# Mixture-of-experts matmuls fed through one shared PSUM bank: two slots per pass instead of one

## The reference

```
xn = layernorm(x)
p  = xn @ Wv.T + bv                      # 16 heads of 8; q = k = v = p
s  = softmax(q k.T / sqrt(8)) v          # per batch and head, 1024 x 1024 scores
s  = s @ Wo.T + bo
z  = layernorm(xn) * g + b               # router and experts see z
w  = top-2 of softmax(z @ rW + rb) over 8 experts, normalised
hid_e = gelu(z @ W1[e] + b1[e])          # 128 -> 256, exact gelu
out_e = hid_e @ W2[e] + b2[e]            # 256 -> 128
f  = xn + sum_e w_e * out_e
out = x + s * silu(f)
```

## Time and profile before

| | us |
|---|---|
| median of 3 runs | 629.17 (628.3 to 630.58) |
| the profiled execution | 632.46 |
| its span | 630.7 |

### The profile page before, as it was taken

The page is one execution under the profiler, slowest core; times in us unless marked ns, Lnnn a source line. Parts: engine busy times, 40 slices in busy tenths (PEclk is TensorE's granted clock), DMA queues, the critical chain, the costliest instruction groups (busy, mean ns, idle before and its releaser), DMA issues.

```text
span 630.7 us, 11527 instructions
## 1 busy us (share of the span) xinstructions
PE 571.2 (91%) x3990; PEld 232.3 (37%) x3990; DVE 240.1 (38%) x695; ACT 543.2 (86%) x591; POOL 230.1 (36%) x252
## 2 busy tenths in 40 slices
PE   3778884799999999799999999999988999999996
PEld 2553320223344344333444344434334343433221
DVE  5553863573333333113222232223232852223381
ACT  4576663699999999979999999999999999999994
POOL 2364047827777774254211121112203334341000
PEclk9977776799999999869999999999995999999999
DMA  6137697746466655227363445453233654442220
GB/s 164 45 101 219 231 304 276 184 132 149 110 162 133 162 96 116 70 67 160 68 153 99 127 112 132 103 135 108 70 117 108 173 167 139 130 116 83 65 66 19
DMA packets 100989, 81.54 MB, mean 129 GB/s; under 512 B 54219, under 2 KB 92638, under 8 KB 100318
## 3 DMA queue, kind: packets, MB, share of 16 engines
q1 hardware_dynamic: 94270, 71.26, 43.2%
q0 software_dynamic: 6656, 9.48, 4.8%
HBM read 58.07 MB, written 28.39 MB: 137 GB/s over the span
## 4 chain that ended last, share of the span: by engine, by line
PE 74%; ACT 9%; DVE 7%; issue 5%; DMA 4%; SPq 1%; ACTq 0%; DVEq 0%
PE bank_v L1330 35%; PE pair L1276 16%; PE bank_f L1370 8%; PE bank_f L1379 8%; ACT exps L776 7%; DMA p_dram<-w_ring 3%; PE bank_f L1347 2%; PE pair L1236 1%; ACT pre L752 1%; PE bank_f L1343 1%; PE pair L1227 1%; DMA x_tok<-in_L_attn_x 1%; DVE o_turned L1082 1%; PE bank_f L1354 1%; DVE v_tok L863 1%
## 5 line engine op out<-in xcount | busy, mean ns | idle before, releaser
L776 ACT ACTIVATE exps<-pair 128x1024 f32<-128x1024 f32 x512 | 488.9, 1049 | 54.6 <-PE pair L1276 36.3
L1330 PE MATMUL bank_v<-exps,v_tok 128*32 128x512 f32 x2048 | 285.0, 630 | 3.1 <-ACT exps L776 1.6
L687 POOL DMA_INDIRECT o_dram<-o_ring,slot_place x80 | 77.4, 968 | 238.3 <-DVE o_ring L1133 238.0
L1276 PE MATMUL pair<-q_ring,k_ring 26*128 26x512 f32 x1024 | 152.9, 513 | 2.7 <-ACT exps L776 2.1
L1276 PEld LDWEIGHTS pair<-q_ring,k_ring 26*128 26x128 f32 x1024 | 60.7, 188 | 93.4 <-ACT exps L776 54.8
L672 POOL DMA_INDIRECT z_dram<-pre,dest_i x64 | 64.3, 1004 | 52.2 <-DVE place_i L1037 33.3
L1379 PEld LDWEIGHTS bank_f<-w_ring,pre 128*128 128x128 f32 x320 | 46.2, 208 | 72.2 <-issue 43.3
L1124 DVE TENSOR_TENSOR pre<-bank_f,w_ring 128x256 f32<-128x256 f32 x80 | 33.9, 423 | 102.1 <-PE bank_f L1370 102.1
L1379 PE MATMUL bank_f<-w_ring,pre 128*128 128x128 f32 x320 | 62.5, 322 | 9.7 <-ACT pre L752 5.3
L1133 DVE TENSOR_TENSOR o_ring<-bank_f,w_ring 128x128 f32<-128x128 f32 x80 | 23.2, 290 | 124.3 <-PE bank_f L1379 121.1
L679 POOL DMA_INDIRECT place_dram<-token_place,place_i x64 | 61.3, 958 | 19.5 <-issue 19.5
(11 more groups left out here) (154 smaller groups left out, 287.1 us busy)
## 6 DMA issues: line engine op xcount, KB each, us to landing
w_ring<-w_dram SPq DMA_DIRECT2D x80, 192.0 KB
w_ring<-w_dram SPq DMA_DIRECT2D x80, 129.0 KB
q_ring<-p_dram SPq DMA_DIRECT2D x56, 104.0 KB
k_ring<-p_dram SPq DMA_DIRECT2D x56, 96.0 KB
z_dram<-s_tok SPq DMA_DIRECT2D x4, 1280.0 KB, 13.1
z_ring<-z_dram SPq DMA_DIRECT2D x80, 64.0 KB
rows_in_sb<-o_dram SPq DMA_DIRECT2D x16, 256.0 KB, 2.9
p_dram<-z_ring SPq DMA_DIRECT2D x8, 256.0 KB, 2.9
```

The lines of the kernel that those rows point to most:

```text
L687: pool.indirect_dma_start(o_dram[:, :], bass.IndirectOffsetOnAxis(slot_place[:, h, 4 * k + i:4 * k + i + 1].bitcast(U32), 0), o_ring[:, q ...
L776: nc.scalar.activation(exps[:, g % ES, 2 * half:2 * half + 2, :], pair[(2 * g + half) % 3][:, :, :], ACT.Exp, scale=SCALE).then_inc(exp_do ...
L1276: ins = nc.tensor.matmul(pair[h % 3][:, j % 2, :], k_ring[32 * j:32 * j + KROWS, n % 2, kt * P:(kt + 1) * P], q_ring[32 * j:32 * j + KROWS ...
L1330: ins = nc.tensor.matmul(bank_v[32 * j:32 * j + 32, :], v_tok[:, (n // HG) * KT + kt, first:first + 32], exps[:, g % ES, j, :], start=(kt ...
```

## The change

A use of the bank now holds two slots of a quad. ("up", q, i) and ("down", q, i) exist for i = 0 and 1 (PAIRS = 2); PE writes both slots one behind the other into different columns of `bank_f` (four calls, eight records), and DVE reads both with one instruction, 128x512 for "up" and 128x256 for "down". `both` places two uses of a quad at a distance of MOE_STEP = 2.52 steps in place of four at 1.19. `burst` puts four uses, all eight slots of two quads, into the step of the gelu, and the next uses may follow three steps later. POOL still stores slot by slot, two stores behind each "down" use. All waits that named the fourth use of a quad now name the second.

```diff
-MOE_STEP = 1.19
+MOE_STEP = 2.52
-BURST = 6
+PAIRS = 2
     def both(kind, q, t):
-        for i in range(4):
+        for i in range(PAIRS):
             t = max(t, place((kind, q, i), t) + 1 - MOE_STEP) + MOE_STEP
         return t
     def burst(first, t):
...
-        downs = [("down", first + i // 4, i % 4) for i in range(8)]
-        uses[g] = downs[:BURST]
+        uses[g] = [("down", first + i // PAIRS, i % PAIRS) for i in range(2 * PAIRS)]
         at.update({what: g for what in uses[g]})
-        t = g + 3
-        for what in downs[BURST:]:
-            t = max(t, place(what, t) + 1 - MOE_STEP) + MOE_STEP
-        return g, t
+        return g, g + 3
...
 (SP, load_w2; load_w1 alike)
-                    sp.wait_ge(bank_f_read, written("down", q - 2, 3))
+                    sp.wait_ge(bank_f_read, written("down", q - 2, PAIRS - 1))
 (POOL, store_o)
-                pool.wait_ge(bank_f_read, written("down", q, i))
+                pool.wait_ge(bank_f_read, written("down", q, i // 2))
 (DVE, read_bank, "up")
-                    ins = nc.vector.tensor_tensor(pre[:, k, i * HF:(i + 1) * HF].rearrange("p (c t) -> p c t", c=FC),
-                                                  bank_f[:, 0:HF].rearrange("p (c t) -> p c t", c=FC),
-                                                  w1_ring[:, q % 2, i, HF:W1W].unsqueeze(2).broadcast_to([P, FC, P]), ALU.add)
+                    ins = nc.vector.tensor_tensor(
+                        pre[:, k, 2 * i * HF:2 * (i + 1) * HF].rearrange("p (s c t) -> p s c t", s=2, c=FC),
+                        bank_f[:, :].rearrange("p (s c t) -> p s c t", s=2, c=FC),
+                        w1_ring[:, q % 2, 2 * i:2 * i + 2, HF:W1W].unsqueeze(3).broadcast_to([P, 2, FC, P]), ALU.add)
 (DVE, read_bank, "down")
-                    ins = nc.vector.tensor_tensor(o_ring[:, q % 2, i, :], bank_f[:, 0:D], w2_ring[:, q % 2, i, FC * D:W2W], ALU.add)
+                    ins = nc.vector.tensor_tensor(o_ring[:, q % 2, 2 * i:2 * i + 2, :], bank_f[:, 0:2 * D].rearrange("p (s d) -> p s d", s=2),
+                                                  w2_ring[:, q % 2, 2 * i:2 * i + 2, FC * D:W2W], ALU.add)
 (PE, write_bank, "up"; "down" alike)
-                    for c in range(FC):
-                        ins = nc.tensor.matmul(bank_f[:, c * P:(c + 1) * P], w1_ring[:, q % 2, i, c * P:(c + 1) * P],
-                                               zT[:, q % 2, i * P:(i + 1) * P], start=True, stop=True)
+                    for a, c in itertools.product(range(2), range(FC)):
+                        slot = 2 * i + a
+                        ins = nc.tensor.matmul(bank_f[:, (a * FC + c) * P:(a * FC + c + 1) * P], w1_ring[:, q % 2, slot, c * P:(c + 1) * P],
+                                               zT[:, q % 2, slot * P:(slot + 1) * P], start=True, stop=True)
```

More of the change, by code:

```diff
@@ L2 @@
+import itertools
 from contextlib import ExitStack
@@ L169, in timetable @@
             order[what] = len(order)
-    load = [at["down", (h + 1) * QUADS - 1, 3] + LOAD_LAG for h in range(HALVES)]
+    load = [at["down", (h + 1) * QUADS - 1, PAIRS - 1] + LOAD_LAG for h in range(HALVES)]
     return uses, at, order, gelu, load
@@ L522, in load_w1 @@
                 if q >= 2:
-                    sp.wait_ge(bank_f_read, written("up", q - 2, 3))
+                    sp.wait_ge(bank_f_read, written("up", q - 2, PAIRS - 1))
                 for a in range(4):
@@ L608, in _ @@
                         load_z(q)
-                    if g == (AT["up", q - 2, 3] + 1 if q >= 2 else MOE_AT - 8 + 2 * q):
+                    if g == (AT["up", q - 2, PAIRS - 1] + 1 if q >= 2 else MOE_AT - 8 + 2 * q):
                         load_w1(q)
-                    if g == (AT["down", q - 2, 3] + 1 if q >= 2 else MOE_AT + 16 + 6 * q):
+                    if g == (AT["down", q - 2, PAIRS - 1] + 1 if q >= 2 else MOE_AT + 16 + 6 * q):
                         load_w2(q)
@@ L698, in _ @@
                     for i in range(4):
-                        if g == AT["down", q, i]:
+                        if g == AT["down", q, i // 2]:
                             store_o(q, i)
@@ L748, in gelu @@
             def gelu(h):
-                act.wait_ge(bank_f_read, written("up", (h + 1) * QUADS - 1, 3))
+                act.wait_ge(bank_f_read, written("up", (h + 1) * QUADS - 1, PAIRS - 1))
                 for k in range(0, QUADS, GELU_QUADS):
@@ L1052, in turn_z @@
                 if q >= 2:
-                    dve.wait_ge(bank_f_written, written("up", q - 2, 3))
+                    dve.wait_ge(bank_f_written, written("up", q - 2, PAIRS - 1))
                 nc.vector.transpose(zT[:, q % 2, :], z_ring[:, q % 2, :]).then_inc(z_turned, 1)
@@ L1377, in write_bank @@
                         pe.wait_ge(gelu_done, h * QUADS // GELU_QUADS + k // GELU_QUADS + 1)
-                    for c in range(FC):
-                        ins = nc.tensor.matmul(bank_f[:, 0:D], pre[:, k, (i * FC + c) * P:(i * FC + c + 1) * P],
-                                               w2_ring[:, q % 2, i, c * D:(c + 1) * D], start=(c == 0), stop=(c == FC - 1))
+                    for a, c in itertools.product(range(2), range(FC)):
+                        slot = 2 * i + a
+                        ins = nc.tensor.matmul(bank_f[:, a * D:(a + 1) * D], pre[:, k, (slot * FC + c) * P:(slot * FC + c + 1) * P],
+                                               w2_ring[:, q % 2, slot, c * D:(c + 1) * D], start=(c == 0), stop=(c == FC - 1))
                 ins.then_inc(bank_f_written, 1)
```

## The result

| | median us | range | ratio to before (95% interval) |
|---|---|---|---|
| before | 629.17 | 628.30 to 631.55 | |
| changed | 634.53 | 633.01 to 637.53 | 1.0083 (1.0046 to 1.0119) |
| changed, run again beside others | 634.68 | 633.27 to 638.17 | 1.0084 (1.0050 to 1.0118) |

The change makes the kernel slower by about 5.2 us (0.0083 x 629.17; 2.9 to 7.5 by the interval). The forecast was 630.5 with 626.0 to 635.5 as its range.

A forecast was written before the change was run, and what follows sets the result against it. PE binds runs of uses, ACT's 1.81 us pace every step. Terms 2.3 - 0.2 - 0.9 - 0.55 + 0.5 + 0.1 = +1.3 us gave 633.7 for the profiled execution; median forecast 630.5, range 626.0 to 635.5.

The forecast's parts named there:

- the lead of 0.20 us: In the loop, PE's lead over ACT is worth 0.20 us; one empty step fills it, and savings beyond are lost.
- PE's saving of 13.7 us: 72 double uses, 0.19 us less PE work each; the rival that this saving pools over steps gave 609 us, chance 4%.
- The double use at 1.09 us: PE time from a two-slot use to the next scores: 0.64 + 0.45 us, 0.19 less than two single uses.
- closer records: Rival: a double use's eight records start 0.08 us apart, not 0.11; 9.4 us less, 621 us, chance 4%.
- The step prices: Steps 38 to 230: double uses cost 0.52 us over ACT's pace behind an empty step, 0.72 behind a use; +2.3 us.
- The wait for `o_turned`: At 499.49 us PE idles because DVE turned the attention output late; the wait goes, -0.55 us, or 0 if another replaces it.
- the first rival: Second slot starts anew (double use 1.28 us, 644 us) or one empty step leaves the lead unfilled (642); partial 633 to 636; 14%.
- The transpose of z: PE's idle time before some quads' first "up": steps 42, 66, 178 before, 42 and 82 after; -0.9 us.
- The bursts: Expert uses under the gelus: four double uses outlast the cover in the second burst, +0.5 us; none taken in the first.
- The tanhs: A tanh delays ACT about 0.5 us, so a use in the same step costs nothing; different uses are covered, -0.2 us.
- The half clock: Behind each gelu the clock is 0.50 for about 17 us; the double use there pays more, +0.1 us.
- The clock as a way to be faster: Rival: fuller bursts keep the clock up; one fall less gives 628 us, both 625.5; chance 12%.

The follow-up runs named there:

- the kernel with one slot: The changed kernel with PE computing only the first slot of each pair, DVE reading its columns twice: 603.46 us, ratio 0.9584 to the kernel before.
- the kernel with split writes: The changed kernel with a pair's two slots written in two successive steps, read together by one DVE instruction: 630.36 us, ratio 1.0010 to the kernel before.
- idle matmuls: Extra matmuls on PE under the gelu: added to the changed kernel, 635.46 us; added to single uses with double ones in the bursts alone, 630.92 us.

## Why the prediction was right or wrong

- **What bounds the kernel, and the lead of 0.20 us: right.** PE's saving of 13.7 us did not pool. This decided the sign, and the double steps of 4.13 us per pair, the kernel with one slot and the kernel with split writes show it from three sides.
- **That the time lay in the range: in part luck.** The effect was forecast at +1.3 us and measured at +5.2, and 633.7 for the profiled execution met 633.01 by chance: it stood on half-clock stretches of 17.1 us, and that execution had 13.7.
- **The double use at 1.09 us, 0.11 between records: right** (1.08). The rivals of a second slot that starts anew (1.28) and of closer records (0.96) are out: the eight weight loads of step 74 cover 0.97 us, and with 0.19 for one the records follow each other after (0.97 - 0.19) / 7 = 0.11 us. The Trainium skill (TensorE: Matmul & The Clock Gate, section Back-to-back issue gap) gives about 81 ns for a matmul of 128 columns with its weight load. For these float32 operands the trace does not agree with it.
- **The step prices, +2.3 us: each right, the sum somewhat low.** 0.52 and 0.72 were measured as 0.52 and 0.70 to 0.78; the up to 0.02 of an empty step was put at nothing, and there are about a hundred of them after.
- **The wait for `o_turned`, -0.55 us: wrong, and this is the step that failed.** The prediction had 0 as its other bound. I read it in the earlier trace rows as one late turn of a busy DVE that would go away. It is a wait that binds wherever PE is early, in every step with g mod 8 = 2 behind an empty one. The nine steps cost 0.92, 0.95, 0.92, 0.97, 0.77, 0.96, 0.76, 0.89 and 0.69, that is 3.15 over nine times 0.52; the forecast had 0.9 of that, as the wait for z in 42 and 82. The other 2.25 less the 0.55 that went: +1.7 in place of -0.55. I had priced the new empty steps as rest without asking what PE would run into when it came early. In these steps the lead is in fact not filled, as in the first rival, but by this wait and not because one empty step is too short. Taking the uses out of them lowers the steps, not clearly the time.
- **The transpose of z, -0.9: about right.** It left steps 66 and 178; 42 and 82 cost 0.40 each over 0.52 (forecast 0.45), shared with the wait above.
- **The bursts, +0.5: right in sum, not in place.** The step behind the first burst, for which nothing was taken, came 0.48 and 0.54 us late in the two executions of the changed kernel (0.02 before); behind the second it was 0.36 and 0.02.
- **The tanhs, -0.2:** no run takes them apart.
- **The half clock, +0.1: wrong in size where it lasts long.** That a double use at half clock pays for both slots was in the working, but for step 92 alone and at the length of one execution. Where the stretch lasts 17.1 us it reaches step 187 too. Steps 88 to 94 and 182 to 192 together, the bursts' delay included, are 0.5 us longer than before with short stretches, 1.4 with long ones (57.64 against 57.12, and 61.16 against 59.75).
- **The clock as a way to be faster: out.** The stretches came as before, and where idle matmuls kept the clock up in the burst it fell behind it.
- **W2 of quad 12, POOL, the wide read: right**, no use waits there outside the bursts.

The sum with the corrected wait is 1.3 + 2.25 = 3.5 us, near the +3.3 of the executions with short stretches, but not term by term. Steps 38 to 88 and 94 to 182 alone lost 4.3 us. For them the forecast's own terms come to 1.9 (step prices +2.7, z -0.84); the seven waits that lie in them add 1.7 (2.6 over 0.52 each, less the 0.9 of z), and the last 0.7 is in the step prices. The last stretch, 192 to 255, gave back 1.1 to 1.7, more than the 0.5 that the terms come to for it with the wait corrected. With long stretches it is +5.3, and the medians' 5.2 lies there. How often each length comes was not measured, so the split of the last 2 us between chance and the half clock stays open.

## What to carry to other kernels

Before joining two pieces of work on one engine, ask how far that engine can run ahead of the one that it feeds: what is saved beyond that lead is lost, and a lump that is longer than the lead makes the fed engine wait although the total work has fallen. Price work by the step in which it stands (behind rest, in a run, under a pause), not by the engine's sum. And when a change makes an engine early, look for the wait that it will meet there, even if that wait costs nothing today.

## What was not expected of the hardware

Without the idle matmuls, the half clock behind a gelu lasted 10.2, 13.7 or 17.1 us in different executions of these kernels (granted clock 0.50), and one kernel's time changes with it by 1 to 2 us per stretch; profiles of single executions should be matched by it before they are subtracted. With the idle matmuls PE was busy for 8.66 of the 9.00 us of the first burst, and the clock there was 1.00; a pause of 3.1 us in which PE worked 0.42 us stood before its next fall.
